# From the first layer's output to the second layer's input: bias row and norm on GpSimd, scaling on ScalarE, an order of VectorE by hand

## What is computed

```python
# L0: grouped-query cross-attention (32 heads of 16, 8 key heads), then a norm over the sum
out = attention0(x, ctx) @ Wo + bo
x = layer_norm(out + x, eps=1e-6) * gamma + beta
# L1: two cross-attentions (16 heads of 128) and an MLP, each behind a norm of its own
for i in (1, 2):
    h = layer_norm(x, eps=1e-5) * scale_i + offset_i
    x = x + cross_attention_i(h, ctx)      # @ wo + bo inside
h = layer_norm(x, eps=1e-5) * scale_mlp + offset_mlp
x = x + gelu(h @ w_fc1 + b_fc1) @ w_fc2 + b_fc2
```

## Time and profile before

| | |
|---|---|
| median of 3 runs | 2627.43 us (2623.31 to 2627.93) |
| the profiled execution | 2627.61 us, its span 2625.8 us |
| TensorE busy | 2360.4 us, 90% of the span |
| VectorE busy | 1515.2 us, 58% |
| ScalarE busy | 1001.8 us, 38% |
| GpSimd busy | 696.2 us, 27% |
| mean granted clock of TensorE | 0.963 |

### The profile page before, as it was taken

One profiled execution on the slowest core, in us unless ns is written; L12 is line 12 of the kernel. 1 busy time (PEld: TensorE's weight loads), 2 busy tenths in 40 slices (PEclk: granted clock), 3 DMA queues, 4 the chain that ended last, 5 costly groups with the idle time before them and its releaser, 6 DMA issues. The chain is left out here.

```text
span 2625.8 us, 36925 instructions
## 1 busy us (share of the span) xinstructions
PE 2360.4 (90%) x13176; PEld 2093.7 (80%) x13176; DVE 1515.2 (58%) x3426; ACT 1001.8 (38%) x2271; POOL 696.2 (27%) x734
## 2 busy tenths in 40 slices
PE   5688699999999999998968876999999999999988
PEld 4555598989989899997756556989899898999977
DVE  4677655555565555556537767555555755555564
ACT  2577242333334233333217762333324333332420
POOL 4021114131331413223541112132231413224045
PEclk8899799999999999999989997999999999999989
DMA  5532123332322332233453221322323232232322
GB/s 185 173 103 59 45 81 113 89 97 77 109 84 82 113 97 89 83 104 120 148 157 99 78 63 52 97 89 85 102 81 105 93 97 89 86 101 86 100 65 82
DMA packets 118891, 253.27 MB, mean 96 GB/s; under 512 B 13648, under 2 KB 37232, under 8 KB 117664
## 3 DMA queue, kind: packets, MB, share of 16 engines
q1 hardware_dynamic: 76504, 140.73, 17.6%
q10 hardware_dynamic: 42208, 110.18, 13.7%
HBM read 222.40 MB, written 31.22 MB: 97 GB/s over the span
## 5 line engine op out<-in xcount | busy, mean ns | idle before, releaser
L652 PE MATMUL pj<-ctx_hi,wk_hi 128*128 128x376 f32 x1088 | 381.9, 351 | 35.8 <-DVE xacc L1372 20.2
L653 PE MATMUL pj<-ctx_lo,wk_hi 128*128 128x376 f32 x1088 | 374.8, 344 | 0.0
L654 PE MATMUL pj<-ctx_hi,wk_lo 128*128 128x376 f32 x1088 | 373.0, 343 | 0.0
L657 PEld LDWEIGHTS tp<-ident,probs 112*125 112x125 f32 (+1 forms) x1536 | 204.0, 170 | 151.8 <-ACT probs L1117 73.3
L1321 DVE TENSOR_TENSOR rr<-pj,rr 128x448 fp32r<-128x448 f32 (+1 forms) x280 | 174.4, 628 | 250.8 <-ACT rr L1011 250.8
L576 POOL TENSOR_SCALAR wk_hi<-raw 128x512 fp32r<-128x512 f32 (+1 forms) x84 | 53.1, 632 | 998.7 <-DMA raw<-in_wk 841.6
L657 PE MATMUL tp<-ident,probs 112*125 112x112 f32 (+1 forms) x1536 | 238.9, 276 | 82.5 <-DVE probs L1603 39.0
L1323 DVE SCALAR_TENSOR_TENSOR k_lo<-pj,cur,k_hi 128x375 fp32r<-128x375 f32 x256 | 155.0, 606 | 248.5 <-ACT k_hi L1013 246.9
L652 PE MATMUL pj<-pt_hi,nat 125*128 125x448 f32 x768 | 287.2, 374 | 6.8 <-issue 5.8
L1013 ACT ACTIVATE k_hi<-pj,cur 128x375 fp32r<-128x375 f32 x256 | 146.5, 572 | 358.5 <-PE pj L654 351.2
L654 PE MATMUL pj<-pt_hi,nat 125*128 125x448 f32 x768 | 282.7, 368 | 0.0
(11 more groups left out here) (172 smaller groups left out, 5354.9 us busy)
## 6 DMA issues: line engine op xcount, KB each, us to landing
nat<-nat_scratch ACTq DMA_DIRECT2D x256, 384.0 KB, 3.7
raw<-in_wk SPq DMA_DIRECT2D x72, 256.0 KB, 3.7
raw<-in_wq SPq DMA_DIRECT2D x72, 256.0 KB, 3.2
raw<-in_wo SPq DMA_DIRECT2D x72, 256.0 KB, 2.6
raw<-in_wv SPq DMA_DIRECT2D x64, 256.0 KB, 3.3
raw<-in_w SPq DMA_DIRECT2D x64, 256.0 KB, 2.9
nat_scratch<-rr SPq DMA_DIRECT2D x8, 1536.0 KB, 7.1
queries_scratch<-rr SPq DMA_DIRECT2D x32, 224.0 KB
```

Of the source, the lines that this page charges most:

```text
L652: nc.tensor.matmul(dst, l_hi, r_hi, start=first, stop=False)
L653: nc.tensor.matmul(dst, l_hi, r_lo, start=False, stop=False)
L654: return nc.tensor.matmul(dst, l_lo, r_hi, start=False, stop=last)
L657: return nc.tensor.transpose(dst, src, ident[0:parts, 0:parts])
```

## The change

VectorE gives up, for the first norm of L1 only: the bias row of L0 (now four additions on GpSimd), `normed` (now four GpSimd instructions that read the same mean and reciprocal), and `scaled` (now ScalarE, straight from PSUM: `x_parts`, eight activations per batch, four that write `h_hi` and four that write the same values into `tmp[1]` for the low part). VectorE keeps the additions from PSUM, all statistics, both instructions with gamma and beta, the reciprocals and the low parts. `group_operands(0)` and `ln_begin` come ahead of the norms, and the four `row_bias` come behind all of them, in a function `l0_norms` that writes VectorE's order out by hand, two or three batches interleaved.

Gamma and beta are loaded into the two slots of `raw`, at head 112 of the 128 of L0's attention, in one DMA that ScalarE's queue issues; GpSimd keeps both slots (`keep=2`) until gamma and beta have been used for the last time, and then frees them for the next weights. TensorE's order of the first units becomes: batch 0, two keys, batch 1, two keys, batches 2 and 3.

```diff
@@ def first_units(a, g):
+    if len(x) == HB:
+        return x[0:1] + keys[0:2] + x[1:2] + keys[2:4] + x[2:4]
...
-    return keys[0:3] + x[0:1] + keys[3:] + x[1:]
+    return keys
+MOMENTS = places([(0, 0), (1, 0), (0, 1), (1, 1), (2, 0), (2, 1), (3, 0), (3, 1)])
@@ GpSimd
-                queries1(0)
+                queries1(0, keep=2)
+                pool.wait_ge(bo_in, hf * 16 + 16)
+                for b in range(HB):
+                    pool.wait_ge(x_in[b], hf * 16 + 16)
+                    nc.gpsimd.tensor_tensor(xa[0:L, b, :], xa[0:L, b, :], tmp[0][0:L, :], ALU.add).then_inc(bias_added, 1)
+                pool.wait_ge(bias_added, hf * 16 + HB)
+                nl = hf * NL
+                for b in range(HB):
+                    pool.wait_ge(ln_inv, nl * HB + b + 1)
+                    if b > 0:
+                        pool.wait_ge(pj_ready, PJ_AT[hf]["g", 0, 0] + GU[0][0]["x", b - 1] + 1)
+                    nc.gpsimd.tensor_scalar(tmp[0][0:L, :], xa[0:L, b, :], mean_var[0:L, b, 0:1],
+                                            rstd[0:L, b:b + 1], ALU.subtract, ALU.mult).then_inc(xn_ready, 1)
+                pool.wait_ge(post_ln, (hf + 1) * 2 * HB)
+                for s in raw_free:
+                    pool.sem_inc(s, 1)
@@ ScalarE
+            def x_parts(nl, b, unit):
+                act.wait_ge(pj_ready, unit + 1)
+                act.wait_ge(ln_par, nl + 1)
+                act.wait_ge(ln_lo, (nl * HB + b) * 2)
+                for k in range(2):
+                    for c in (2 * k, 2 * k + 1):
+                        nc.scalar.activation(h_hi[:, c, b * L:(b + 1) * L], pj[unit % PJ][:, c * L:(c + 1) * L],
+                                             ACT.Identity, bias=ln_cur[:, 4 + c:5 + c], scale=ln_cur[:, c:c + 1])
+                    for c in (2 * k, 2 * k + 1):
+                        i = nc.scalar.activation(tmp[1][:, c * L:(c + 1) * L], pj[unit % PJ][:, c * L:(c + 1) * L],
+                                                 ACT.Identity, bias=ln_cur[:, 4 + c:5 + c], scale=ln_cur[:, c:c + 1])
+                    i.then_inc(ln_hi, 1)
...
+                    if n == NT - 16:
+                        act.wait_ge(w_ready["b"], (hf * WB_H + B_G + 1) * DC)
+                        act.dma_start(raw[0:L, :, :], rows_in[0:1, D:3 * D].partition_broadcast(L).rearrange(
+                            "p o (r n) -> p (o r) n", r=2)).then_inc(rows_ready, 16)
...
-                act.dma_start(probs_flat[0:L, D:3 * D],
-                              rows_in[0:1, D:3 * D].partition_broadcast(L)).then_inc(rows_ready, 16)
-                for b in range(HB):
-                    ln_std(hf * CHAIN_H + 2 * b + 1, slice(b, b + 1), 0)
-                    ln_stds(hf * NL, b)
...
+                        post_std(hf, 0)
+                        post_std(hf, 1)
+                        ln_stds(nl, 0)
+                        ln_stds(nl, 1)
+                        post_std(hf, 2)
+                        x_in_place(0)
+                        keys1(0, 0)
+                        ln_stds(nl, 2)
+                        post_std(hf, 3)
+                        keys1(0, 1)
+                        x_in_place(1)
+                        ln_stds(nl, 3)
+                        keys1(0, 2)
+                        keys1(0, 3)
+                        x_in_place(2)
+                        x_in_place(3)
...
-                act.wait_ge(post_ln, hf * 2 * HB + 2 * HB)
                 rows_of(0)
@@ VectorE: the loop of four batches (L1539 to L1563) and ln_begin and normed(nl, 0) in attend go out
+                    def rest(b):
+                        dve.wait_ge(ln_hi, (nl * HB + b) * 2 + 2)
+                        dve.wait_ge(pj_free, gpj + gu["x", b] + PJ)
+                        dve.sem_inc(pj_free, 1)
+                        h_rest(nl, b)
...
+                    ln_begin(nl, 0)
+                    added(0)
+                    moments_of(0, 0)
+                    post_normed(0)
+                    added(1)
+                    moments_of(1, 0)
+                    added(2)
+                    moments_of(0, 1)
+                    inverse(0)
+                    post_normed(1)
+                    added(3)
+                    moments_of(1, 1)
+                    moments_of(2, 0)
+                    inverse(1)
+                    rest(0)
+                    post_normed(2)
+                    keys1(0)
+                    moments_of(2, 1)
+                    moments_of(3, 0)
+                    keys1(1)
+                    inverse(2)
+                    post_normed(3)
+                    rest(1)
+                    moments_of(3, 1)
+                    keys1(2)
+                    inverse(3)
+                    keys1(3)
+                    rest(2)
+                    rest(3)
+                    for b in range(HB):
+                        dve.wait_ge(xn_ready, nl * HB + b + 1)
+                        row_bias(b, hf * 64 + 32)
+
                 group_operands(0)
+                l0_norms()
```

More of the change, by code:

```diff
@@ L567, in _, with split_free @@
                 pool.sem_inc(s, 1)
-            def split_free(n, shape, hi, lo, signal, k, done):
+            def split_free(n, shape, hi, lo, signal, k, done, keep=False):
                 slot = n % 2
@@ L579, in split_free, with weights @@
                 pool.wait_ge(signal, done)
-                pool.sem_inc(raw_free[slot], 1)
-            def weights(n, name, free, use):
+                if not keep:
+                    pool.sem_inc(raw_free[slot], 1)
+            def weights(n, name, free, use, keep=0):
                 pool.wait_ge(w_free[name], free + 1)
@@ L625, in _, with queries1 @@
                 weights(base + RAW_W0, "o", hf * WO_H, hf * WO_H)
-                def queries1(ag):
-                    weights(base + RAW_A + ag * RAW_GU + DC, "b", use_b + B_G + 2 * ag, use_b + B_G + 2 * ag)
+                def queries1(ag, keep=0):
+                    weights(base + RAW_A + ag * RAW_GU + DC, "b", use_b + B_G + 2 * ag, use_b + B_G + 2 * ag, keep)
                 def keys1(ag):
@@ L1015, in move, with post_std @@
                     i.then_inc(mid, 1)
-            def ln_std(chain, batches, which):
-                act.wait_ge(ln_chain, chain)
-                nc.scalar.activation(std[0:L, batches], mean_var[0:L, batches, 1], ACT.Sqrt,
-                                     bias=eps[0:L, which:which + 1]).then_inc(std_ready, 1)
+            def post_std(half, b):
+                act.wait_ge(ln_chain, half * HB + b + 1)
+                nc.scalar.activation(std[0:L, b:b + 1], mean_var[0:L, b:b + 1, 1], ACT.Sqrt,
+                                     bias=eps[0:L, 0:1]).then_inc(std_ready, 1)
+            def x_parts(nl, b, unit):
[10 more added lines that the diff above has]
+                    i.then_inc(ln_hi, 1)
             def ln_stds(nl, b):
@@ L1226, in attend, with x_in_place @@
                     act.wait_ge(cur_ready, hf * CUR_H + a * G1 + g + 1)
-                    for name in first_units(a, g):
+                    if a == 0 and g == 0:
+                        def x_in_place(b):
+                            x_parts(nl, b, gpj + gu["x", b])
+                        post_std(hf, 0)
[14 more added lines that the diff above has]
+                        x_in_place(3)
+                    for name in first_units(a, g) if a + g > 0 else []:
                         if name[0] == "k":
@@ L1340, in normed @@
                 half, i = divmod(nl, NL)
-                dve.wait_ge(std_ready, half * STD_H + (2 * b + 2 if i == 0 else (i + 1) * HB + b + 1))
+                dve.wait_ge(std_ready, half * STD_H + (i + 1) * HB + b + 1)
                 nc.vector.reciprocal(rstd[0:L, b:b + 1], std[0:L, b:b + 1]).then_inc(ln_inv, 1)
@@ L1536, in _ @@
                 out0(NT // 8 - 1)
-                dve.wait_ge(bo_in, hf * 16 + 16)
-                for b in range(HB):
-                    dve.wait_ge(x_in[b], hf * 16 + 16)
-                    nc.vector.tensor_tensor(xa[0:L, b, :], xa[0:L, b, :], tmp[0][0:L, :], ALU.add).then_inc(bias_added, 1)
-                    dve.wait_ge(bias_added, hf * 16 + b + 1)
-                    out_part(at["w0"], b, b, pad=3 if b == HB - 1 else 1)
-                    chain, norm = hf * CHAIN_H + 2 * b, hf * 2 * HB + 2 * b
-                    dve.wait_ge(stats_ready, hf * ST_H + 2 * b + 1)
-                    dve.sem_inc(dve_passed, 1)
-                    nc.vector.bn_aggr(mean_var[0:L, b, :], stats[0:L, b, :]).then_inc(ln_chain, 1)
-                    dve.wait_ge(ln_chain, chain + 1)
-                    if b == 0:
-                        dve.wait_ge(rows_ready, hf * 64 + 16)
-                    nc.vector.scalar_tensor_tensor(xa[0:L, b, :], xa[0:L, b, :], mean_var[0:L, b, 0:1],
-                                                   tmp[1][0:L, :], ALU.subtract, ALU.mult).then_inc(post_ln, 1)
-                    dve.wait_ge(std_ready, hf * STD_H + 2 * b + 1)
```

(15 more changed lines are left out.)

43 lines of the change are left out of this document (40 added, 3 removed).

## The result

| | before | after |
|---|---|---|
| median of the runs made beside each other | 2627.93 us (15 runs) | 2617.89 us (15 runs) |
| ratio, 95% interval | | 0.996 (0.9943 to 0.9977) |
| the profiled execution, its span | 2627.61, 2625.8 us | 2610.48, 2608.7 us |
| passage, first half | 41.20 us | 35.67 us |
| passage, second half | 40.24 us | 36.01 us |

The two medians lie 10.0 us apart, and the interval of the ratio puts the gain between 6 and 15 us. The prediction had 12.0 and 2615.4 us. "Passage" is, as there, the time from the start of the first bias addition to the start of the first query matmul. The two passages became 5.53 + 4.23 = 9.76 us shorter; 12.4 were forecast.

A forecast was written before the change was run, and what follows sets the result against it. TensorE, the busiest engine, waits for VectorE in the passage. Shortening it to 34.5 us saves 6.7 + 5.7 = 12.4 us, minus 0.4 for the DMA: 12.0, median 2615.4 us; 8 in 10 range 2606 to 2625.

The forecast's parts named there:

- The bound and the place: Passage before the first query matmul: TensorE waits for VectorE 17.8 us in one half; time won there should last.
- First part: Passage up to batch 3's addition from PSUM, forecast done at 13.25 us, with TensorE resuming at 13.3 us.
- Blocking: GpSimd and VectorE instructions in the passage hold each other; passage 34.5 us with this rule, 31.9 without.
- GpSimd's norm: L1's first norm, mean and reciprocal as per-row scalars: 0.65 us taken from L576's 0.62, bounds 0.55 and 1.3.
- if a GpSimd form takes over twice its nearest row: Sign that the prediction is wrong; nearest rows were 1.28 us for the bias addition, 0.62 for the norm.
- ScalarE's activations: Scale and offset from PSUM, 128x112: 0.24 us from start to start, 2.0 per batch of eight; bounds 0.12 and 0.34.
- The last two batches: End of passage: batch 2's activations from 28.85 us, batch 3's end at 33.7, last low part done at 34.45.
- the 13.1 us: VectorE's work leaving the 41.2 us passage: additions, scalings and norms 10.2, the rest group 0 operands and row_bias.
- the new hand-offs eat the gain: Rival: activations at 0.34, additions 1.6, norms 1.3 make the passage 39.4 us, total 2625.7; chance 0.13.
- The DMA for gamma and beta: ScalarE issues it inside L0's attention: 0.2 us per half, bounds 0 and 0.45, minus 0.4 in all.
- The held slots: Late release of raw delays wo loads and splits in group 0; hidden with some 3 us left, priced at nothing.
- The key units: TensorE's 12 matmuls per key: 2.07 us at full clock, 3.8 at half; first key counted at half clock.

## Why the prediction came out as it did

**The bound and the place: right.** The time was won in the passage, TensorE's 9.4 us wait went, and nothing in group 0 took it back: the kernel after has no wait of TensorE for `wo` or `wv`.

**The size: right in sum, with terms off in both directions.** The forecast passage was 34.5 us, the measured ones 35.67 and 36.01. That the sum came so near is in part luck: activations priced 2.9 us per half too low stand against a first part priced 1.3 too long, in a kernel whose gain came mostly from elsewhere (below).

- *First part, forecast too long.* The prediction had the last addition from PSUM done at 13.25 us; it was done 11.9 us behind the first bias addition (287.40 less 275.48). Of these 1.3 us the increments are about 0.5 (three of the eight pairs of statistics, 1.4 us in all, lie ahead of it; I had worked with the old distances), and 0.7 us had been won when batch 0's multiplication by beta was done, 6.0 us behind the start for my 6.7: blocking priced too high in this half. TensorE went on at 12.1 us (287.62); what released it was GpSimd's first norm, done at 287.57, not the addition that the prediction named.
- *Blocking: the mechanism right, its price not constant.* Beside GpSimd's bias additions the multiplication by gamma took 1.20 us and the one by beta 0.80 in the first half, 1.57 and 1.41 in the second, where undisturbed ones take 0.75; I had written up to 1.2 us longer. What I missed of it is GpSimd's splits of `wo`: priced at nothing, since `row_bias` and casts had room, they also run beside the last low parts. These took 1.11 and 0.85 us for 0.69. Here that is 0.6 us; in the runs where GpSimd was free earlier it was over 2.
- *GpSimd's norm: mis-sized.* Priced at 0.65 us, bounds 0.55 to 1.3; it takes 2.07 undisturbed. The nearest row, L576, is a TENSOR_SCALAR of nearly the same size (0.62 us) without per-row scalars, and it misled. The prediction had said that it is wrong "if a GpSimd form takes over twice its nearest row"; by that test it is, though its time came out. The step did little harm: with the norms on VectorE and undisturbed low parts the passage is within 0.3 us of this one (35.43 and 35.79), though doubling shows about two of the four norms on the path.
- *ScalarE's activations: mis-sized.* 0.33 us from start to start for 0.24. I counted three batches on the path; the run with twelve activations shows all four there. 32 times 0.09 are 2.9 us per half.
- *The last two batches* carry both: 8.0 us for 5.6. ScalarE began them at 27.4 us, 1.5 us ahead of my 28.85; the query matmul started 0.3 us behind the last low part, for 0.05. 2.4 - 1.5 + 0.25 is the 1.2 us by which the first passage is longer than the forecast; the second is 1.5 us longer.

**The credit: wrong.** Of the 13.1 us that the prediction took from VectorE's part of a passage, 10.2 were work moved to other engines and 2.9 work moved out of the passage, and it saw the gain mainly in the first. The run with the order alone, which has the 2.9 and the dropped increments but not the 10.2, has 9.2 of the 9.8 us of the two passages. Beside it, moving the bias additions and the norm to GpSimd wins 3.2 us in the first half and 3.0 in the second (32.83 and 33.16 for 36.07 and 36.14), and moving the scaling to ScalarE, eight instructions for four in a chain through one buffer, gives 2.8 back in each. So the rival "the new hand-offs eat the gain" has its mechanism in the runs, but not its size: what the scaling costs eats what the other two moves bring, and the order carries the result without them.

**The rest.** The DMA for gamma and beta was issued at head 112 as forecast, at 245.89 us, for 0.34 us of ScalarE's queue:

```profile
245.89 0.34 ACTq L1203 DMA_DIRECT2D raw<-in_rows  x1
```

Its price of 0.2 us per half can't be told from the spread of executions and stays open. The held slots made TensorE wait for no weights, as argued: GpSimd's next split after those of `wo` waits 6.83 us for ScalarE's release, where I had left some 3 us of room:

```profile
323.16 0.62 POOL L586 TENSOR_SCALAR wb_hi<-raw 128x512 fp32r<-128x512 f32 x1 [6.83 <-ACTq L1303]
```

The key units: the first one began at half clock as counted, and the clock rose within it. Windows of the kernel after (columns as in the earlier trace rows):

```profile
288.30:290.90 2.60, 2.60 (x10) 2.60 (x9) 0.72 (x3) 2.10 (x8) 1.74 (x1) 0.50 0.02 6
291.20:293.20 2.00, 2.00 (x13) 2.00 (x12) 1.01 (x3) 1.28 (x4) 0.04 (x1) 1.00 0.00 0
```

TensorE had done nothing between the end of L0's product (its last matmul ended at 285.4) and the transposes at 287.62. At 1.2 GHz (0.50) a matmul of a key starts every 0.31 us, at 2.4 GHz every 0.17.

## What to carry to other kernels

When one engine's serial chain keeps another waiting, look first at its order: what of it can stand ahead of the stretch or behind it, what frees the waiting engine's buffers, and which bare semaphore increments can go. Measure that alone, before moving work to other engines: here it was nearly all of the gain, though the runs don't say how much of it each of the three was. A move pays if the other engine does it in no more instructions and beside the chain; it loses if the work is split into twice as many small ones that take turns with the next step through one buffer. And when work is moved or held back on GpSimd, look also at what it will do next, and beside which VectorE instructions that falls.

## What the runs showed of the hardware that I had not expected

- GpSimd's TENSOR_SCALAR with two per-row scalars of 112x512 takes 2.07 us, its TENSOR_SCALAR of 128x512 without them 0.62 us; VectorE does the first in 0.55.
- That GpSimd instruction holds VectorE for only a part of its time. Both timelines of the kernel after:

```profile
285.73 1.07 DVE L1773 SCALAR_TENSOR_TENSOR xacc<-xacc,prm,raw 112x512 f32<-112x512 f32 x1
286.72 0.68 DVE L1432 TENSOR_TENSOR xacc<-pj,xacc 112x512 f32<-112x512 f32 x1
```

  The norm ran from 285.15 to 287.57 (ends on GpSimd are rough in this profile). The multiplication with beta beside it lost 0.32 us and ended at 286.80, while the norm still ran, and the addition from PSUM was not held at all. Beside GpSimd's TENSOR_TENSOR of the bias row the same multiplication lost 0.66 us (second half, 1.41 for 0.75). "SBUF — State Buffer" of the Trainium skill (Who interferes with whom) has GpSimd and VectorE share a port pair as an exclusive lock; the additions and splits here agree with it, the norm shows that such an instruction need not keep VectorE out until it ends.
- Bare semaphore increments in VectorE's queue are not free: sixteen per passage were 1.1 to 1.4 us.
- An activation of 128x112 from PSUM with scale and bias from SBUF starts every 0.33 us; the instruction behind one of 128x375 starts after 0.45 (296.78 to 297.23). Over three times the elements add 0.12 us, so by this estimate the small ones are mostly fixed cost; the two forms aren't quite alike, since the long one reads a bias alone.
